# Attention with a 130-key last tile: the two tail keys' share of the value sums added on VectorE instead of in TensorE pieces

## The reference: cross attention with layer norm modulation

```python
xq  = ada_ln(x_q,  t_vec, Wss_q,  bss_q)      # x_q: 1 x 4096 x 512
xkv = ada_ln(x_kv, t_vec, Wss_kv, bss_kv)     # x_kv: 1 x 3202 x 512
q = (xq @ Wq + bq).reshape(B, Lq, 16, 32)
kv = (xkv @ Wkv + bkv).reshape(B, Lkv, 2, 16, 32)
k, v = kv[:, :, 0], kv[:, :, 1]
scores = jnp.einsum('bqhd,bkhd->bhqk', q, k) / jnp.sqrt(jnp.float32(32))
attn = jax.nn.softmax(scores, axis=-1)
out = jnp.einsum('bhqk,bkhd->bqhd', attn, v).reshape(B, Lq, 512)
return x_q + (out @ Wp + bp)
```

## Time and profile before

| | |
|---|---|
| median of 3 runs | 2204.33 us (2203.1 to 2204.34) |
| the profiled execution | 2204.24 us, its span 2202.5 us |
| granted TensorE clock in it | 0.999 |
| busy: TensorE products, weight loads | 2167.0 us (98%), 628.5 us (29%) |
| busy: VectorE, ScalarE, GpSimd | 1895.3 us (86%), 1820.7 us (83%), 29.7 us (1%) |
| DMA | 180.92 MB, mean 82 GB/s |

### The profile page before, as it was taken

The page is one execution under the profiler, slowest core; times in us unless marked ns, Lnnn a source line. Parts: engine busy times, 40 slices in busy tenths (PEclk is TensorE's granted clock), DMA queues, the critical chain, the costliest instruction groups (busy, mean ns, idle before and its releaser), DMA issues.

```text
span 2202.5 us, 56645 instructions
## 1 busy us (share of the span) xinstructions
PE 2167.0 (98%) x25378; PEld 628.5 (29%) x25378; DVE 1895.3 (86%) x1095; ACT 1820.7 (83%) x1908; POOL 29.7 (1%) x29
## 2 busy tenths in 40 slices
PE   7999999999999999999999999999999999999997
PEld 3444322222222222222222222222222222222222
DVE  2312799989999899999999999989999999989997
ACT  1211799999999999999999999999999999989994
POOL 0000000000000000000000000000000000000000
PEclk9999999999999999999999999999999999999999
DMA  7322321224222422223222422233222322232211
GB/s 267 129 88 88 116 72 55 66 59 127 61 69 68 118 61 65 71 64 116 70 65 65 115 75 63 58 92 98 70 60 71 96 76 59 66 101 66 55 47 56
DMA packets 171434, 180.92 MB, mean 82 GB/s; under 512 B 14000, under 2 KB 117168, under 8 KB 171184
## 3 DMA queue, kind: packets, MB, share of 16 engines
q1 hardware_dynamic: 171184, 177.22, 26.9%
HBM read 146.27 MB, written 30.92 MB: 80 GB/s over the span
## 4 chain that ended last, share of the span: by engine, by line
PE 96%; DMA 2%; DVE 1%; issue 1%; ACT 0%; SPq 0%; POOL 0%
PE bank L662 38%; PE bank L674 35%; PE bank L593 5%; PE bank L750 4%; PE bank L704 4%; PE bank L605 4%; PE bank L715 1%; PE bank L686 1%; DMA arena<-l_recip 1%; PE bank L574 1%; PE bank L812 1%; PE bank L726 1%; DMA arena<-in_ctx_dram 0%; DVE arena L1112 0%; DMA l_recip<-r_blk 0%
## 5 line engine op out<-in xcount | busy, mean ns | idle before, releaser
L907 ACT ACTIVATE arena<-bank,shift 128x1024 f32<-128x1024 f32 x1600 | 1692.2, 1113 | 162.7 <-PE bank L662 156.0
L1179 DVE TENSOR_TENSOR arena<-arena 128x2048 f32<-128x2048 f32 x736 | 1670.0, 2289 | 113.6 <-ACT arena L907 100.8
L662 PE MATMUL bank<-qs,ks 32*64 32x512 f32 x12800 | 922.2, 613 | 1.1 <-ACT arena L871 0.7
L674 PE MATMUL bank<-arena,vg 128*32 128x512 f32 x6400 | 852.3, 605 | 1.3 <-ACT arena L907 1.3
L674 PEld LDWEIGHTS bank<-arena,vg 128*32 128x32 f32 x6400 | 125.9, 108 | 650.6 <-ACT arena L907 648.2
L662 PEld LDWEIGHTS bank<-qs,ks 32*64 32x64 f32 x12800 | 206.8, 129 | 346.8 <-ACT arena L907 204.5
L750 PE MATMUL bank<-wp,arena 128*32 128x168 f32 (+2 forms) x2464 | 153.7, 321 | 1.7 <-DVE arena L1112 1.7
L704 PE MATMUL bank<-xt,wq 128*32 128x256 f32 x1792 | 137.7, 379 | 0.0
L750 PEld LDWEIGHTS bank<-wp,arena 128*32 128x32 f32 x2464 | 79.9, 110 | 186.8 <-issue 170.2
L1057 DVE TENSOR_TENSOR arena<-bank,bv_b 128x512 f32<-128x512 f32 (+1 forms) x26 | 18.0, 691 | 131.5 <-PE bank L605 131.4
L871 ACT ACTIVATE arena<-bank,bk_c 128x512 f32<-128x512 f32 (+1 forms) x28 | 18.0, 642 | 135.7 <-PE bank L593 135.7
(11 more groups left out here) (86 smaller groups left out, 429.3 us busy)
## 6 DMA issues: line engine op xcount, KB each, us to landing
ks<-k_full SPq DMA_DIRECT2D x160, 320.0 KB, 3.1
vg<-v_full SPq DMA_DIRECT2D x160, 320.0 KB, 3.8
xin<-in_x_dram SPq DMA_DIRECT2D x8, 1024.0 KB, 10.1
q_full<-qs SPq DMA_DIRECT2D x32, 256.0 KB, 2.1
arena<-in_x_dram SPq DMA_DIRECT2D x8, 1024.0 KB, 10.2
out_dram<-arena SPq DMA_DIRECT2D x32, 256.0 KB, 2.1
arena<-l_recip SPq DMA_DIRECT2D x28, 256.0 KB, 5.9
arena<-in_ctx_dram SPq DMA_DIRECT2D x6, 1024.0 KB, 7.8
```

The source lines that it names most:

```text
L662: mm = nc.tensor.matmul(bank[out, 2 * (i % RING) + h % 2, :], ks[rows_of(h), keys], qs[rows_of(h), g, :], start=True, stop=True)
L674: mm = nc.tensor.matmul(bank[rows_of(h), o_bank(u), :], vg[:, t, rows_of(h)], pt[t % PR][:, h, :], start=(t == 0), stop=False, skip_group_ ...
L907: nc.scalar.activation(pt[t % PR][:, 2 * pair:2 * pair + 2, :], bank[:, first:first + 2, :], ACT.Exp, scale=SCALE, bias=shift[:, g:g + 1]) ...
L1179: nc.vector.tensor_tensor(a[:, :, :], (pt[t - 1] if k <= 2 else a)[:, :, :], pt[t % PR][:, :, :], ALU.add).then_inc(p_added, 1)
```

## The change

`weigh_tail` is gone, with both of its pieces in each unit. `take_sums` waits for the last `weigh` of its unit (`pv_done`) in place of the job. In its stead:

- SyncE loads the block's tail exponentials of each unit back from `pt_dram` (`load_tail`): four DMAs, one for each head of the group, each spreads the two rows of the head over 32 partitions into the one buffer `p_b`. It stands behind the third of the five key and value loads of the next unit (`load_kv(u + 1, 2)`) and waits for the stores of the tail and for the additions of the unit before.
- VectorE does two instructions of 128x512 for each unit (`add_tail`), behind the adds of steps 3 and 4 of the next unit: `o_mid = p_b[0] * vt[0] + o_all`, then `o_all = p_b[1] * vt[1] + o_mid`. `o_mid` lies in the memory of `bss_b`, which is no longer used then.
- `vt` holds the two tail rows of the values by column (128 x 4 x 2) and is loaded by two DMAs whose elements are single numbers; its clearing on GpSimd is gone.
- `divide` and the last division wait for `tail_added` instead of the copied sums. `JOB`'s numbers for `job_taken` stay; `job_done` gets numbers without the `"o"` jobs (`DONE`).

```diff
@@ -265,9 +269,12 @@
                                 jobs.extend(("q", b + 1, g - 1, i) for i in range(2))
                         jobs.append(("o", u))
                 jobs.append(("l", UNITS - 1))
-                return {job: n for n, job in enumerate(jobs)}
-
-            JOB = schedule()
+                return jobs
+
+            JOBS = schedule()
+            JOB = {job: n for n, job in enumerate(JOBS)}
+
+            DONE = {job: n for n, job in enumerate(job for job in JOBS if job[0] != "o")}
 
             def o_bank(u):
                 return 6 + u % 2
...
@@ -359,6 +366,16 @@
                             n = HG * TAIL
                             sp.dma_start(pt_dram[g * n:(g + 1) * n, b * QB:(b + 1) * QB],
                                          p_tail[g * DH:g * DH + n, :]).then_inc(pt_out, 16)
+
+                    def load_tail(u):
+                        b, g = divmod(u, NG)
+                        sp.wait_ge(pt_out, 16 * NG * (b + 1))
+                        if u > 0:
+                            sp.wait_ge(tail_added, TAIL * u)
+                        for h in range(HG):
+                            row = (g * HG + h) * TAIL
+                            sp.dma_start(p_b[rows_of(h), :, :], pt_dram[row:row + TAIL, b * QB:(b + 1) * QB].unsqueeze(0)
+                                         .broadcast_to([DH, TAIL, QB])).then_inc(pb_in, 16)
 
                     def load_l(b, heads):
 
...
@@ -454,12 +471,9 @@
                             load_kv(0, 3)
                     stored(KB - 1)
                     load_kv(0, 4)
-                    sp.wait_ge(consts, 5)
-                    for g in range(NG):
-                        for h in range(HG):
-                            row = g * DH + h * TAIL
-                            sp.dma_start(vt[row:row + TAIL, g, rows_of(h)],
-                                         v_dram[NT * P:LKV, g * P + h * DH:g * P + (h + 1) * DH]).then_inc(vt_in, 16)
+                    for k in range(TAIL):
+                        sp.dma_start(vt[:, :, k], v_dram[NT * P + k, :].rearrange("(g p) -> p g", p=P),
+                                     allow_slow_non_contiguous=True).then_inc(vt_in, 16)
 
                     for b in range(NB):
                         for g in range(NG):
...
@@ -491,6 +505,7 @@
                                 store_tail(b)
                             if more:
                                 load_kv(u + 1, 2)
+                            load_tail(u)
                             if g == 0 and b + 2 < NB:
                                 load_x(b + 2)
                             if g > 0 and b > 0:
...
@@ -675,19 +689,6 @@
                                                   pt[t % PR][:, h, :], start=(t == 0), stop=False, skip_group_check=True)
                         mm.then_inc(pv_done, 1)
 
-                    def weigh_tail(u, half):
-
-                        b, g = divmod(u, NG)
-                        cols = halves_of(half)
-                        pe.wait_ge(job_taken, JOB["p", b] + 1)
-                        if u == 0:
-                            pe.wait_ge(vt_in, 16 * NH)
-                        for h in range(HG):
-                            mm = nc.tensor.matmul(bank[rows_of(h), o_bank(u), cols], vt[:, g, rows_of(h)],
-                                                  p_tail[:, cols], start=False, stop=True, skip_group_check=True)
-                        if half == 1:
-                            mm.then_inc(job_done, 1)
-
                     def free(job):
 
                         if JOB[job] > 0:
...
@@ -769,8 +770,6 @@
                             turn_queries(u, b + 1, max(t - 11, 0))
                         if t == 11:
                             tail_scores(u, b)
-                        if t in (15, 24):
-                            weigh_tail(u, t // 24)
 
                     def later_side(u, b, g, t):
                         if b > 0:
...
@@ -787,8 +786,6 @@
                                 project_queries(u, b + 1, g - 1, 0, t - 14)
                             if 18 <= t < 22:
                                 project_queries(u, b + 1, g - 1, 1, t - 18)
-                        if t in (22, 24):
-                            weigh_tail(u, t // 24)
 
                     pe.wait_ge(fills, 1)
                     scores(0, 0)
...
@@ -944,7 +941,7 @@
 
                     def take_sums(u):
                         b, g = divmod(u, NG)
-                        finished(("o", u))
+                        act.wait_ge(pv_done, NT * (u + 1))
                         if b > 0:
                             act.wait_ge(on_ready, b)
                         nc.scalar.activation(o_all[:, g, :], bank[:, o_bank(u), :], ACT.Copy).then_inc(job_taken, 1)
...
@@ -1104,11 +1101,25 @@
                         dve.wait_ge(r_done, b + 1)
                         nc.vector.reduce_max(l_tops[rows, 1, b:b + 1], r_blk[rows, :], AX_X).then_inc(l_step, 1)
 
+                    def add_tail(u, k):
+
+                        g = u % NG
+                        if k == 0:
+                            dve.wait_ge(pb_in, 16 * HG * (u + 1))
+                            dve.wait_ge(vt_in, 16 * TAIL)
+                            dve.wait_ge(job_taken, JOB["o", u] + 1)
+                            src, dst = o_all[:, g, :], o_mid[:, :]
+                        else:
+                            dve.wait_ge(tail_added, TAIL * u + 1)
+                            src, dst = o_mid[:, :], o_all[:, g, :]
+                        nc.vector.scalar_tensor_tensor(dst, p_b[:, k, :], vt[:, g, k:k + 1], src, ALU.mult, ALU.add
+                                                       ).then_inc(tail_added, 1)
+
                     def divide(b, groups):
                         dve.wait_ge(r_in, 16 * HG * (b + 1))
-                        dve.wait_ge(job_taken, JOB["o", NG * b + groups - 1] + 1)
+                        dve.wait_ge(tail_added, TAIL * (NG * b + groups))
                         if b > 0:
-                            dve.wait_ge(job_done, y_last(b - 1, TPB - 1) + 1)
+                            dve.wait_ge(job_done, DONE[y_last(b - 1, TPB - 1)] + 1)
                         nc.vector.tensor_tensor(on[:, 0:groups, :], o_all[:, 0:groups, :], r_b[:, 0:groups, :], ALU.mult
                                                 ).then_inc(on_ready, 1)
 
...
@@ -1178,6 +1189,8 @@
                             a = sums[(k - 1) % 2]
                             nc.vector.tensor_tensor(a[:, :, :], (pt[t - 1] if k <= 2 else a)[:, :, :], pt[t % PR][:, :, :],
                                                     ALU.add).then_inc(p_added, 1)
+                            if u > 0 and t in (3, 4):
+                                add_tail(u - 1, t - 3)
                             if g == 0:
                                 first_side(b, t)
                             else:
...
@@ -1187,9 +1200,12 @@
                                                 ).then_inc(p_added, 1)
 
                     last = NB - 1
+                    for k in range(TAIL):
+                        add_tail(UNITS - 1, k)
                     dve.wait_ge(job_taken, JOB["l", UNITS - 1] + 1)
                     nc.vector.reciprocal(r_sb[:, :], l_sb[:, :]).then_inc(r_done, 1)
                     dve.wait_ge(r_done, NB + 1)
+                    dve.wait_ge(tail_added, TAIL * UNITS)
                     nc.vector.tensor_tensor(on[:, NG - 1, :], o_all[:, NG - 1, :], r_sb[:, :], ALU.mult
                                             ).then_inc(on_ready, 1)
                     dve.wait_ge(xy_ready, NB)
```

25 lines of the change are left out of this document (14 added, 11 removed).

## The result

The changed kernel takes **2193.87 us** (median of 5 runs, 2192.8 to 2195.27) against 2203.1 us of the kernel before on the same chip (5 runs, 2202.64 to 2204.34): ratio 0.9956 [0.9943, 0.9969], faster by 0.3 to 0.6%. Two later measurements of the same kernel gave 2194.24 and 2193.5 us, ratios 0.996 [0.9945, 0.9975] and 0.9946 [0.9932, 0.9959]. The forecast was 2194.2.

The account below looks back on a forecast made before the run. The bound was taken as a loop of TensorE and ScalarE, not one full engine. Borders from g > 0 give 3.6 + 6.5 = 10.1 us, other terms 0: 2202.5 to 2192.4 us of span, 2194.2 us predicted, range 2186 to 2201.

Parts of the forecast that it names:

- The loop of two engines: TensorE and ScalarE hold each other; without a piece, steps alternate 2.04 and 2.38 us, 2.49 with `take_sums` between.
- the walk: Intervals followed through one g = 3 border, both pieces out: 0.51 us gained there, 0.41 at g = 1 and 2.
- g = 0 gives nothing: At borders from g = 0 units ScalarE holds both places, so removing both pieces gives 0.
- VectorE's additions: Two new instructions a unit, 0.69 us each with 0.60 of queue; late at step 5, on time by step 8; cost 0.
- The last unit: VectorE's two new instructions, 1.4 us, fall into its 2.71 us wait for ScalarE's `l_sb`; earlier exponentials give 0 too.
- SyncE and DMA: Four 128 KB loads a unit, wanted some 30 us after issue, with nothing new ahead of the reciprocals' transfer; cost 0.
- `vt` by number: Slow load of 1024 single-number descriptors, nearest row 11.0 us; over 50 us until unit 1, so nothing waits.
- Full price of the pieces: Rival: each of 64 pieces gives its full 0.43 us of TensorE time, 27.5 us, to 2176.8; chance 0.05.
- The eaten gain: Rival: additions above 1.0 us each make VectorE late at `invert` in g = 0 units, 4 to 10 us, 2198 to 2204; chance 0.10.
- The case between: Rival: the 2.04 and 2.38 alternation falls out of step, 0.26 a piece, 12 to 18 us, 2186 to 2192; chance 0.15.
- VectorE as bound: Rival: from about 1.5 us an instruction VectorE becomes the bound and the kernel slower, about 2300; chance 0.04.
- Nothing at all: Rival: pieces vanish but ScalarE holds every border as at g = 0, leaving 2204; chance 0.05.

Follow-up runs that it names:

- experiment 2: Kernel before without the earlier tail piece of each unit (step 22, or 15 for g = 0), the one of step 24 kept: 2196.93 us, ratio 0.9965.
- experiment 3: Kernel before without the later tail piece of each unit (step 24), the one of step 22 or 15 kept: 2198.32 us, ratio 0.9974.
- experiment 8: Changed kernel with ScalarE's copy of the value sums done twice, the first into unread memory: 2208.81 us, ratio 1.0021.
- experiment 4: Kernel before without both tail pieces in the units with g = 0 only: 2202.98 us, ratio 0.9999.
- experiment 1: Changed kernel without its two VectorE additions and the four tail loads of each unit: 2197.02 us, ratio 0.997.
- the two repeats: The changed kernel measured again, unchanged, beside other experiments: 2194.24 and 2193.5 us.
- experiment 7: Changed kernel with each of the two VectorE additions done twice, the first into unread memory: 2201.04 us, ratio 0.9987.
- experiment 9: Changed kernel with experiment 5's load move, and output pieces, `invert` and `divide` one step earlier at g = 0: 2191.01 us, ratio 0.9939.
- experiment 5: Changed kernel with the residual's 1 MB load moved behind the tail's load on SyncE's queue: 2194.0 us, ratio 0.9957.
- experiment 6: Kernel before with the residual's load moved behind `load_kv(u + 1, 2)`: 2203.95 us, ratio 1.0.

## Why the prediction was right, point by point

- **The loop of two engines.** Right. Steps of 2.04, 2.38 and 2.49 in the profile after; the walk's 10.33 us measured as 10.33; 0.40 and 0.49 per border against 0.41 and 0.51. Experiments 2 and 3 show that the two pieces of a unit don't add up (0.41 and 0.32 alone, 0.40 together), and experiment 8 shows what holds the border now. The walk was of one border of seven, though, and its 0.51 for unit 15 (measured 0.21) was too much.
- **g = 0 gives nothing.** Right for six of the seven units with b > 0 (experiment 4 has the same zeros). Unit 12 gave 0.25 one step behind the border, in experiment 4 too and in none with the second piece left in (experiment 2). Unit 0 was in the same sentence, but it has no output pieces and so no copy of one near its border: it gave 0.31, in experiment 4 too. A reading of one border was carried to units that it does not fit.
- **VectorE's additions.** The term was 0.69 us for an instruction with 0.60 of queue; it is 0.747 with 0.67. It costs nothing either way. On time by step 9, not 8. VectorE in unit 17 is busy for 59.59 of 60 us and ScalarE does not wait for it in that window: of its five buffers enough stay free, and experiment 1 without any addition has the same borders.
- **The last unit.** Right: the reciprocal after the last add 2.72 us late as before, the additions in its idle time (1.26 left of 2.71).
- **SyncE and DMA.** Cost 0 within what can be told. The loads landed in 4.1 us, the reciprocals' in 5.6 (5.9 before). The sum of VectorE's waits for them rose from 10.7 to 11.9 us; of single blocks, up to 1 us in either direction. SyncE's long issue of a reciprocal load in block 1 is in all three profiles of the changed kernel (3.02, 2.95 and 2.51 us) and in experiment 8 (3.01), but also in experiment 1 (2.67), which has none of the tail's loads; in the kernel before the longest is 1.46. So the tail's loads are not needed for it, and its cause stays open. TensorE's idle time at that place was 1.53, 0.80 and 0.51 us in the three profiles, so it cost little.
- **`vt` by number.** Named as slow, with the bias column's 11.0 us as nearest row; it landed in 3.4. The row was of a load at the start, where the page shows 267 GB/s in the first fortieth of the span; that the traffic made it slow is not shown. Neither matters.
- **The rivals.** Full price of the pieces: out by experiment 1. The eaten gain: a true mechanism that begins between 1.3 and 2.7 us a unit. The case between: out by the borders, since it needs 0.52 for two pieces at each border from g > 0, and 16 of them gave 0.40. VectorE as bound: not reached even with 2.7 us a unit (+6.8 us where an added bound would give about 42). Nothing at all: true of g = 0 only.
- **The sum** was 2192.4 of span, measured 2192.2, 2190.4 and 2192.1. That it meets to 0.2 us in the first profile is partly luck: unit 0 sooner by 0.5, its border's 0.3 and unit 12's 0.25 stand against 0.5 more in the divisions and 0.3 less at unit 15. In the two repeats it is luck of another kind: the first exponential was 2.4 us sooner than in the kernel before, for which the sum has no term, and 1.7 and 1.5 us went back in the end stage, where the clock fell. The loop's 10 us are shown, the meeting of the totals to 0.2 us is not.

## What to carry to other kernels

An engine that is busy for 98% can be held by another one: write the loop as a recurrence with the waits of its ring, walk it through once with the piece out, and price a removed piece by what the walk gives, not by its duration. Gains of neighbouring pieces don't add: here the first was worth 0.41 and the second 0.00 to 0.06 us. Work moved to an engine with slack is free only until its lateness meets something on a deadline, here the reciprocals in step 10, so look for the first such step behind it and count what the steps up to there give back.

## What the runs showed of the hardware

- A `scalar_tensor_tensor` of 128x512 float32 takes 0.747 us where a `tensor_tensor` of that size takes 0.685.
- TensorE's granted clock can fall in the middle of a run after it has stood. In the third profile of the changed kernel it stood 2.81 us for a division in block 7:

```profile
1964.70 0.23 PEld L751 LDWEIGHTS bank<-wp,arena 128*32 128x32 f32 x8 [2.81 <-issue]
```

```profile
1964.50:1968.50 4.00, 3.77 (x32) 0.88 (x36) 4.00 (x3) 0.63 (x1) 0.00 (x0) 0.57 0.74 196
```

The granted clock over these 4 us was 0.57, so most of them were at 1.2 GHz. In the first profile the same place had stood 2.67 us and kept 1.00; from tile 10 to tile 24 that unit was 1.7 us shorter, and only 0.14 of it is the standing. The same happened in the end stage of the profiles of experiments 1 to 4, 7 and 9 and of both repeats, for 3.4 or 6.8 us, where TensorE had stood 2.8 to 4.7 us for the last sums (in experiment 1, 8 products of 128x512 took 1.9 us where they took 1.1), and not in the profiles of the kernel before, of the first changed one and of experiments 5, 6 and 8, which had stood 2.8 to 3.4 us there. What decides is open. From the last exponential to the end of the span the eight with the fall took 34.4 to 36.7 us and the five without it 32.6 to 33.7.
- The exponentials of equal kernels start up to 2 us apart: TensorE came to its lasting full clock at 22.6 to 24.4 us in seven profiles, whose exponentials start at 231.9 to 232.6 us, and at 28.1 to 29.6 in six, with 233.8 to 234.8. This may not be chance alone: of the eight profiles of kernels built on the changed one seven are early, of the five built on the kernel before none. The change takes the clearing of `vt` on GpSimd out of the kernel, but no run tried that by itself, so whether some 2 us of its gain arise there is open. An effect of 2 us has to be read inside the profile, at the place where it arises, and not from the total.
